# Cross attention and routed FFN in float32: the transposed x read from the host, its mean sent round by POOL, and another order of work where the weight chunks turn

## The reference

```python
def _L0_xattn_ref(query, key):                 # per batch: 224 x 2048, 750 x 2048
    a = jnp.einsum('bqd,bkd->bqk', query, key)
    e = jax.nn.softmax(a, axis=-1)
    return jnp.einsum('bqk,bkd->bqd', e, key)

def _L0_ffn_ref(x, base_w, base_b, A, B, router_w):
    base_out = jnp.einsum('bsi,oi->bso', x, base_w) + base_b
    res_hidden = jnp.einsum('bsi,ri->bsr', x, A)           # r = 64
    probs = jax.nn.softmax(jnp.einsum('bsi,ei->bse', x, router_w), axis=-1)   # 16 experts
    topw, topi = jax.lax.top_k(probs, 2)
    topw = topw / (jnp.sum(topw, axis=-1, keepdims=True) + 1e-06)
    combine = jnp.sum(jax.nn.one_hot(topi, 16) * topw[..., None], axis=-2)
    delta = jnp.einsum('bse,bsr,eor->bso', combine, res_hidden, B)
    return base_out + delta * 0.5

x = x + _L0_xattn_ref(_layernorm(x), ctx_4096)
x = x + _L0_ffn_ref(_layernorm(x), base_w, base_b, A, B, router_w)
```

## Time and profile before

| what | value |
| --- | --- |
| time, median of 3 runs | 1387.13 us (1379.29, 1387.13, 1390.94) |
| the profiled execution, its own time | 1381.78 us |
| its span (first to last instruction) | 1380.0 us |
| granted TensorE clock, mean | 0.996 |
| busy PE, DVE, ACT, POOL | 98%, 68%, 45%, 22% |
| DMA | 345.34 MB, mean 250 GB/s |

### The profile page before, as it was taken

The page is one execution under the profiler, slowest core; times in us unless marked ns, Lnnn a source line. Parts: engine busy times, 40 slices in busy tenths (PEclk is TensorE's granted clock), DMA queues, the critical chain, the costliest instruction groups (busy, mean ns, idle before and its releaser), DMA issues.

```text
span 1380.0 us, 17969 instructions
## 1 busy us (share of the span) xinstructions
PE 1346.1 (98%) x6777; PEld 1104.9 (80%) x6777; DVE 937.2 (68%) x1193; ACT 625.8 (45%) x777; POOL 310.3 (22%) x233
## 2 busy tenths in 40 slices
PE   5999999999999999999999998999999999999998
PEld 4768888887878888786888886887888888888887
DVE  5577778778777878868556376777776664464644
ACT  3455655545555554555411366787785211111110
POOL 2001102020200202020614742445542111111110
PEclk9999999999999999999999999999999999999999
DMA  8967868787877868869756688999984978878785
GB/s 295 285 215 246 247 233 248 240 277 242 263 218 256 260 215 261 263 213 218 245 179 169 208 246 266 288 347 309 331 274 153 335 240 255 259 248 281 250 270 163
DMA packets 160248, 345.34 MB, mean 250 GB/s; under 512 B 51680, under 2 KB 68064, under 8 KB 145760
## 3 DMA queue, kind: packets, MB, share of 16 engines
q1 hardware_dynamic: 141600, 277.06, 64.8%
q0 software_dynamic: 10528, 52.85, 11.9%
q10 hardware_dynamic: 8064, 14.68, 3.0%
HBM read 260.87 MB, written 99.41 MB: 261 GB/s over the span
## 4 chain that ended last, share of the span: by engine, by line
PE 87%; DMA 7%; DVE 3%; issue 1%; ACT 1%; SPq 0%; POOL 0%; ACTq 0%; POOLq 0%; DVEq 0%
PE scores L887 13%; PE scores L889 13%; PE scores L888 13%; PE scores L753 6%; PE scores L755 6%; PE scores L754 6%; PE scores L856 6%; PE scores L858 6%; PE scores L857 6%; DMA y_scratch<-y_out,yrow_i 4%; PE work L790 3%; DMA x<-in_x_dram 2%; PE work L923 2%; PE work L924 2%; DMA w_in<-in_wT_dram 1%
## 5 line engine op out<-in xcount | busy, mean ns | idle before, releaser
L887 PE MATMUL scores<-w_h,a_h 128*128 128x512 f32 x896 | 351.9, 393 | 0.0
L889 PE MATMUL scores<-w_h,a_l 128*128 128x512 f32 x896 | 350.9, 392 | 0.0
L888 PE MATMUL scores<-w_l,a_h 128*128 128x512 f32 x896 | 350.4, 391 | 0.0
L1091 ACT ACTIVATE a_h<-a_in 128x512 fp32r<-128x512 f32 x148 | 83.6, 622 | 315.6 <-DMA a_in<-xT_scratch 213.0
L889 PEld LDWEIGHTS scores<-w_h,a_l 128*128 128x128 f32 x896 | 168.3, 188 | 37.8
L888 PEld LDWEIGHTS scores<-w_l,a_h 128*128 128x128 f32 x896 | 168.4, 188 | 37.0
L887 PEld LDWEIGHTS scores<-w_h,a_h 128*128 128x128 f32 x896 | 168.3, 188 | 36.9 <-DVE w_l L1461 0.2
L1470 DVE TENSOR_TENSOR a_l<-a_in,a_h 128x512 fp32r<-128x512 f32 x148 | 105.5, 759 | 123.3 <-ACT a_h L1091 119.6
L1223 DVE TENSOR_TENSOR raw_l<-raw_in,val_h 128x512 fp32r<-128x512 f32 x192 | 155.5, 827 | 47.5 <-ACT val_h L1017 46.7
L753 PE MATMUL scores<-ctxT_h,nT_h 128*112 128x494 f32 (+1 forms) x512 | 174.8, 341 | 1.1 <-DVE nT_l L1209 1.1
L755 PE MATMUL scores<-ctxT_h,nT_l 128*112 128x494 f32 (+1 forms) x512 | 172.2, 336 | 0.0
(11 more groups left out here) (150 smaller groups left out, 1990.7 us busy)
## 6 DMA issues: line engine op xcount, KB each, us to landing
ctxT_in<-in_ctxT_dram SPq DMA_DIRECT2D x64, 750.0 KB, 7.8
raw_in<-in_ctx_dram SPq DMA_DIRECT2D x32, 1280.0 KB
a_in<-xT_scratch SPq DMA_DIRECT2D x37, 1024.0 KB, 8.2
w_in<-in_wT_dram SPq DMA_DIRECT2D x32, 512.0 KB, 8.9
x<-in_x_dram SPq DMA_DIRECT2D x8, 1792.0 KB, 10.0
y_add<-y_scratch SPq DMA_DIRECT2D x56, 256.0 KB, 7.1
late_y<-y_scratch SPq DMA_DIRECT2D x56, 256.0 KB, 6.7
xn<-in_x_dram SPq DMA_DIRECT2D x7, 1792.0 KB, 15.3
```

The costliest lines, as they stand in the source:

```text
L887: pe.matmul(o, ah, wh, start=(k == 0), stop=False)
L888: pe.matmul(o, ah, wl, start=False, stop=False)
L889: last = pe.matmul(o, al, wh, start=False, stop=(k == KD - 1))
```

## The change

- **Query from the host.** The host also hands over `xT`, x transposed. SP loads it straight into `xT_in`, which lies over `nT_l` (`load_xT`), after batch b's `hid` job and after POOL has read the old contents (`xT_staged`). There are no "qT" jobs in stages "first" and "mid", no `normalise(xn, ...)` on ACT, no transposes on PE. Only the first batch is still done in the old way ("pre").
- **Mean.** The transposed x is centred by DVE: `centre` subtracts from four blocks the mean of each row, laid out along the columns of every partition (`mean_b`). POOL makes `mean_b` (`spread_mean`): it stores the means (2 x 224 numbers) to DRAM, loads them back broadcast to 128 partitions, and packs every second number. The first of these steps waits for `aggr1`, each later one for the one before.
- **Scale.** The reciprocal deviation is not applied to the query; it scales the scores: the row maximum is multiplied by it on DVE (one more small instruction after each `reduce_max`, with `max_step` between), and the exponential takes it as its scale.
- **Places.** Statistics at e = 4 to 7, two each; mean at e = 8; `centre` of parts 0 and 1 at e = 16 and 18 and of parts 2 and 3 at j = 2 and 4 of the next batch's scores; the high parts at e = 18, 20 and j = 3, 5; the low parts at e = 19, 22 and j = 3, 5. PE waits for part j/2 at pair j.
- **Rows.** `xn` and `x2` alternate as `rows[b % 2]`; the row load serves both the statistics and the residual, so each x row is read once in this layout. In a mid batch it is issued after all four x2T transposes of the batch. In the first stage both row loads go before the loads of the next keys.
- **Loop.** PE, ACT and DVE run the six mid batches unrolled.
- **Turn of the chunks.** `Y_TILES` gives tile 13 one expert (it had two), behind k = 2; every later expert is one place later, and the last falls on tile 27. In tile 14 the pairs 6 and 7 are converted behind the `rows_out` of the tile's first expert, not ahead of it. POOL's `add_bias(29)` stands behind the last scatter.

```diff
-LN1_AT = (9, 10)
-QT_AT = (13, 14, 16, 17)
+STATS_AT = (4, 5, 6, 7)
+MEAN_AT = 8
+CENTRE_AT = (16, 18)
+X_HIGH_AT = (18, 20)
+X_LOW_AT = (19, 22)
...
-        for g in range(TT - 2, 2 * TT - 1):
-            count = min(2 if g in (TT - 1, TT) else 3, SL - n)
+        for g in range(TT - 2, 2 * TT):
+            count = min({TT - 1: 1, TT: 2}.get(g, 3), SL - n)
...
-        Y_BEHIND = {2: (4, 11), 3: (3, 8, 13)}
+        Y_BEHIND = {1: (2,), 2: (4, 11), 3: (3, 8, 13)}
...
+            def load_row(b):
+
+                sp.dma_start(rows[b % 2][:, :, :], x_v[b]).then_inc(row_loaded[b % 2], 16)
+
+            def load_xT(b):
+                sp.dma_start(xT_in[:, :, :], xT[b]).then_inc(xT_loaded, 16)
...
                     sp.wait_ge(filled, job_no(stage, b, "x2T", NX - 1) + 1)
-                sp.dma_start(x2[:, :, :], x_v[b]).then_inc(xres_loaded, 16)
                 if not last:
+                    if not first:
+                        load_row(b + 1)
                     score_done(sp, b, NPC - 1)
                     load_ctxT(b + 1, LR - 1)
+                    if not first:
+                        sp.wait_ge(filled, job_no(stage, b, "hid") + 1)
+                        sp.wait_ge(xT_staged, b * NX)
+                    load_xT(b + 1)
                     raw_again(b, 0)
...
-                    if stage != "last" and e in QT_AT:
-                        pe.wait_ge(ln1_done, b * NQ + NQ)
-                        transpose_rows(stage, b, "qT", xn, QT_AT.index(e))
...
+            def x_high_part(b, n):
+                act.wait_ge(centred, (b - 1) * NX + n + 1)
+                act.activation(four_blocks(nT_h, n), four_blocks(xT_in, n), ACT.Copy).then_inc(x_high, 1)
...
+                dve.reduce_max(nraw[:, q:q + 1], all_scores(q), AX.X, negate=True).then_inc(max_step, 1)
+                dve.wait_ge(rstd1, b + 1)
+                dve.wait_ge(max_step, (b - 1) * NQ + q + 1)
+                dve.tensor_tensor(nmax[:, q:q + 1], nraw[:, q:q + 1], rs1[:, q:q + 1],
+                                  ALU.mult).then_inc(max_ready, 1)
+
+            def centre(b, n):
+
+                if n == 0:
+                    dve.wait_ge(xT_loaded, b * 16)
+                    dve.wait_ge(mean_ready, b)
+                cut = slice(4 * n, 4 * n + 4)
+                dve.tensor_tensor(xT_in[:, cut, :], xT_in[:, cut, :],
+                                  mean_b.unsqueeze(1).to_broadcast([P, 4, LQ]), ALU.subtract).then_inc(centred, 1)
+
+            def x_low_part(b, n):
+                dve.wait_ge(x_high, (b - 1) * NX + n + 1)
+                dve.tensor_tensor(four_blocks(nT_l, n), four_blocks(xT_in, n), as_f32(four_blocks(nT_h, n)),
+                                  ALU.subtract).then_inc(x_ready, 1)
...
+            def spread_mean(b):
+
+                pool.wait_ge(aggr1, b * NQ + NQ)
+                pool.dma_start(mean_d[b], mv1[:, :, :]).then_inc(mean_stored, 16)
+                pool.wait_ge(mean_stored, b * 16)
+                pool.dma_start(mean_in, mean_d[b].rearrange("p q s -> (p q s)").unsqueeze(0).to_broadcast([P, 2 * LQ])
+                               ).then_inc(mean_loaded, 16)
+                pool.wait_ge(mean_loaded, b * 16)
+                at_least(pool, centred, (b - 1) * NX)
+                pool.tensor_copy(mean_b.rearrange("a (q p) -> a q p", q=NQ),
+                                 mean_in.rearrange("a (p q s) -> a q p s", q=NQ, s=2)[:, :, :, 0]
+                                 ).then_inc(mean_ready, 1)
```

More of the change, by code:

```diff
@@ L162, in xattn_ffn_kernel @@
         "pre": group("qT", NX),
-        "first": group("eT", NQ) + group("qT", NX),
-        "mid": BEFORE + group("eT", NQ) + OLD + group("qT", NX),
+        "first": group("eT", NQ),
+        "mid": BEFORE + group("eT", NQ) + OLD,
         "last": BEFORE + group("eT", NQ) + OLD,
@@ L262, in xattn_ffn_kernel @@
             assert nc.sbuf_base <= SBUF_END
+        rows = [xn, x2]
+        mean_in = bias_b[:, 0, 0:2 * LQ]
+        mean_b = bias_b[:, 1, 0:LQ]
         at_w = nc.sbuf_base
@@ L530, in one @@
                     raw_again(b - 1, CH - 1)
[L531 to L535, removed]
                 if not last:
                     if first:
+                        load_row(1)
                         sp.wait_ge(filled, job_no("pre", 0, "qT", NX - 1) + 1)
-                    else:
-                        sp.wait_ge(filled, job_no("mid", b, "x2T", 0))
-                    sp.dma_start(xn[:, :, :], x_v[b + 1]).then_inc(xn_loaded, 16)
+                        sp.dma_start(xn[:, :, :], x_v[0]).then_inc(xres_loaded, 16)
                     for j in range(LR - 1):
@@ L949, in _ @@
             one(0, "first")
-            with pe.Fori(1, NB - 1) as b:
+            for b in range(1, NB - 1):
                 one(b, "mid")
@@ L1027, in one @@
                     ctx_high(b, j)
+                    if stage != "first" and j in (3, 5):
+                        x_high_part(b, 2 + (j - 3) // 2)
                     if stage == "first" and j in (2, 3):
@@ L1121, in _ @@
             one(0, "first")
-            with act.Fori(1, NB - 1) as b:
+            for b in range(1, NB - 1):
                 one(b, "mid")
@@ L1190, in _ @@
                             weight_high((c + 1) * PAIRS + j)
+                    if i == 0 and s == Y_TILES[g][0]:
+                        for j in range(6, PAIRS):
+                            weight_high(c * PAIRS + j)
                     if s + 2 < SL:
@@ L1413, in one @@
                     x2T_low(NX - 1)
-                if new and old:
-                    dve.wait_ge(xn_loaded, b * 16 + 16)
-                    for i in range(4):
-                        stats(xn, st1, stat1, i)
                 for q in range(NQ):
@@ L1559, in _ @@
             one(0, "first")
-            with dve.Fori(1, NB - 1) as b:
+            for b in range(1, NB - 1):
                 one(b, "mid")
@@ L1622, in _ @@
                             weight_low((c + 1) * PAIRS + j)
+                    if i == 0 and s == Y_TILES[g][0]:
+                        for j in range(6, PAIRS):
+                            weight_low(c * PAIRS + j)
                     if s + 2 < SL:
```

133 lines of the change are left out of this document (79 added, 54 removed).

## The result

The changed kernel takes 1394.74 us (median of 14 runs, 1389.66 to 1399.81) against 1380.35 us before (14 runs beside it): ratio 1.0079 [1.0061, 1.0097]. I had said 1354 us, within 1341 to 1376. The measured time lies outside, and the sign is wrong as well: 14.4 us slower by the medians and 0.8% by the ratio, where I forecast 26 us less.

What follows compares the result with a forecast made beforehand. PE, busy 98% of the span, was taken as the bound. -21.8 - 2.9 - 8.0 + 3.5 = -29.2 us against the profiled 1381.78 gave 1352.6, put at 1354 us since the runs' median lies higher; range 1341 to 1376.

Steps and rivals of the forecast that it cites:

- Transposes removed: Stages first and mid: 28 groups of qT transposes leave PE, 0.78 us each, saving 21.8 us.
- First batch: Values of the first batch: earlier row load and spread statistics save 3.4 us, xT load costs 0.5; sum -2.9 us.
- Row, centring, scores: Work added to values and scores: row late by 0.2 us, centring 1.0 us, scores 0.5 us per batch, +3.5 us in all.
- DVE and ACT are not full: Denies the rival that DVE and ACT are full, costing 10 to 14 us: 1366 us, chance 0.10.
- Mean: Values of a batch: two DMAs from POOL at 3.2 us each and a 0.6 us copy, mean ready at 244.0.
- The due time: Values of batch 2: the mean may come up to 245.4, 1.3 us of delay free, each further one paid seven times.
- the mean comes late, at the pace of the hn store: Rival, values: 5.6 us per DMA, mean ready at 248.8, seven times 24 us, so 1378 us; chance 0.11.
- POOL held up by DVE: Rival, mean's steps on POOL: each up to 1 us late behind a DVE instruction, 11 us, 1365 us; chance 0.06.
- Turn: Turn of the chunks: PE's 5.23 us stall and 2.8 us of lower clock go, saving 8.0 us.
- The sum: Whole kernel: the terms add to -29.2 us against the profiled 1381.78 us, giving 1352.6 us.
- The rule of the Trainium skill: DMA engines take turns between queues packet by packet; by it the mean's DMAs pass SP's backlog and the sum stays.

Runs made afterwards that it cites:

- e6: Changed kernel with the mean spread by two small products on PE, new turn kept, run once more: 1355.73 us, 0.9796 of before.
- e4: Changed kernel with the mean spread by PE into a PSUM bank, without the mean's DMAs and POOL's copy: 1356.26 us, 0.9814 of before.
- e3: Changed kernel with `centre` subtracting zeros and not waiting for the mean, DMAs and copy still done: 1355.68 us, 0.9797 of before.
- e7: Changed kernel with SP's x2T store of a mid batch issued only once the mean has come back: 1363.47 us, 0.9866 of before.
- e8: Changed kernel with the mean's store and load issued by ACT, only the copy left to POOL: 1376.40 us, 0.9942 of before.
- e10: Changed kernel with the x2T store packed into one DMA, runs of 14 KB, FFN loads picking columns in small runs: 1445.79 us, 1.0450.

## Why the prediction was wrong

By its own steps:

- **Transposes removed, 28 groups of 0.78 us: right.** The mid batch shown for `e6` is 76.6 us, in the middle of the 76.2 to 76.9 that I gave; the mean of six is 76.7 in `e4` and 77.0 in `e6`. The first product of the FFN starts at 633.0 us in `e4`, 636.2 in `e3` and 636.5 in `e6`, where my terms put it at 635.5. The earlier trace rows were enough.
- **First batch, -2.9 us: right, but hidden.** With the mean on PE the values of batch 0 take 35.4 us against 41.8 before: 6.4 less, where 4 x 0.78 + 2.9 is 6.0. In the changed kernel the mean took it back by a gap of 3.1 us and a lower clock.
- **Row, centring, scores, +3.5 us of slack lost: about right in size.** 79.3 - 3.12 = 76.18, and 76.6 was measured in `e6`, of which 0.4 us are the two small products. So centring and scores took nothing that shows in such a batch. What did cost something was the row, which I had at 0.2 us: it landed late in batch 2 of `e6` (2.46 us of DVE's time, row above), a batch that took 1.7 us more. Over the six batches the mean is 0.5 (`e4`) to 0.8 us (`e6`) above 76.18, where I had 0.5. DVE and ACT are not full.
- **Mean: the step that failed.** "I take 3.2 us each, nearer to rows 10, since POOL has a queue to itself." The start was right (root at 235.9 said, 236.29 seen), and 3.2 is not far off for engines that are little used (3.6 us in `e7`). But the trip begins just when SP stores x2T and loads value blocks, and there each DMA took 5.0 to 8.3 us. The mean was ready at 250.1 instead of 244.0. Of my two reference rows the wrong one was nearer: the store of hn at 5.6 us lies in the same stretch, and it was in the right company, which matters, not in the right queue, which doesn't (`e8`). The profile of before would have told: asked for that stretch it says

```profile
231.00:237.00 6.00, 6.00 (x27) 4.51 (x26) 5.22 (x13) 4.47 (x6) 1.10 (x1) 1.00 0.34 101
237.00:243.00 6.00, 6.00 (x28) 4.51 (x27) 3.41 (x7) 4.20 (x6) 0.00 (x0) 1.00 1.05 287
```

  DMA engines a third busy up to 237, and full behind it. I had moved the mean's start from the first row into the second (4 us later, by my own step on the row load) and did not look at what else is there.
- **The due time: 1.6 us too early.** I said 245.4, from DVE's work up to the end of the values (the items that I name there add to 14.0 us, not 13.3). The rows say 247.0, and another reason: PE stood 3.13 us when the mean came at 250.1, and 0.37 us when it came at 247.5 (`e8`, batch 2). What runs out first is the value block behind `centre` in DVE's program, which PE wants at 248.9.
- **The rival "the mean comes late, at the pace of the hn store": right mechanism, too small.** It had 5.6 us each, 24 us and 1378, and 0.11. The gaps were 23.9 us, but that they agree is luck: with the mean at 248.8, as it had it, and the due time that the rows give, it would have come to some 13 us (an estimate, 7 x 1.8). The DMAs were slower than 5.6 us, and the due time later. What it left out was the clock: behind five of the seven gaps it is at its lower level (1.2 GHz of 2.4, the products 0.43 us apart) for a while, up to 11.6 us more. I had counted this for the turn and not for stalls that the change adds. And it took the 8 us of the turn as given.
- **"POOL held up by DVE": not seen in the changed kernel.** The root took 1.08 us, as before; the copy 0.56 (0.6 said). But DVE stood waiting for that very copy. In `e7`, where DVE was still at work when the copy of batch 2 began, it took 1.20 us (row above), and 0.92 to 1.42 us in five of seven batches. That DVE's instructions held it there was not tried.
- **Turn, -8.0 us: a term from one execution, the second that was mis-sized.** 3.9 and 3.7 us by two comparisons, nothing by a third (1394.87 against 1394.74 us). I took the stall from the profile in which it was the largest of four (5.23, 4.17, 2.37 and 0.73 us), and gave the new order of the experts no price: in tile 23 it meets DVE.
- The sum with these put in: 1352.6 + 23.9 (gaps) + 10.9 (clock behind them) + 6.8 (second part) = 1394.2, against 1394.51. It closes by construction, since 10.9 and 6.8 are what the measured starts leave over; only the 23.9 are added up from rows. Of the 6.8, 4.1 to 4.3 us are the turn (8.0 less the 3.9 and 3.7 of the pairs of runs); the rest is no more than what one execution differs from another, for the changed kernel again took 5.5 us less in this part.

The rule of the Trainium skill, "DMA: Bandwidth & Descriptors", section "Queues, rings and completion order", that an engine takes turns between its queues packet by packet, was read too hopefully. From it one may draw that a small DMA does not wait for another queue's whole backlog, and the trace agrees, with 6 us for the mean's where a piece of 1024 KB of the x2T store takes 10.9 (median); but not that it is free of that backlog. The rise from 3.6 to 6.1 us is measured here. That the packed store makes it worse (8.5 us) would fit turns by packets, but no run here shows that this is the reason.

## What to carry over

A small DMA on the critical chain costs what the DMA engines' load at its moment makes of it, whoever issues it: read the DMA share of the very stretch, at the time to which the change moves it, before choosing a reference row. When a stall is possible, price the clock behind it too, as the rows behind the stalls already there show it. And a term that is one wait of one execution wants a second profile, or a range of its own.

Where a value of 1.8 KB has to reach all partitions while the engines are busy with bulk, two small products on PE (four matmul instructions of 112 columns, 0.27 us each, 0.4 us of PE's time together) did it in place of a trip of 12.3 us (237.3 to 249.6 us in batch 2), and made the kernel 1.9 to 2.0% faster than before instead of 0.8% slower.

## What the runs showed of the hardware that I had not expected

- The same 1.8 KB store lands in 3.5 us where the DMA engines are 39% busy (`e7`, the share in batch 2), in 6.4 us beside a store in runs of 128 to 512 B with the engines full (the changed kernel), and in 8.5 us behind one with runs of 14 KB (`e10`); medians of seven.
- For the mean's store and load together, ACT's queue and POOL's gave nearly the same landings: median 6.2 and 6.1 us.
- Stalls of PE of 3.1 to 3.8 us in the values (batches 2, 4 and 5) were followed by a granted clock of 0.91 over 18 us, of which the products 0.43 us apart are the trace; those of 3.1 us in batch 0 and 5.9 us in batch 3 by 0.84 over 21 us. Behind the ones of 2.7 us (batch 1) and 2.0 us (batch 6) the clock stayed at 1.00. What decides between them stays open.
- Why DVE's emptying of expert 30 is late was read from the timeline, and not tried.
